# Cross-attention on one core: where the row-maximum steps stand in the score phase

## What is computed

```
qn = layernorm(x);  q = qn @ Wq / 8;  k, v = split(media @ Wkv)      # 16 heads of 64
sim  = where(mask, q @ k.T, lowest)                                   # 256 x 1601 for each head
attn = softmax(sim);  x = x + tanh(gate) * (attn @ v) @ Wo
x = x + tanh(ff_gate) * gelu(layernorm(x) @ W1) @ W2
# second layer: softmax attention over the raw media, a sigmoid gate, an RMS norm
```

## Time and profile before

| | |
|---|---|
| median of 3 runs | 872.42 us (lowest 872.27, highest 2096.33) |
| span of the profiled execution | 870.5 us; the time around it is not listed apart |
| TensorE matmul busy | 833.8 us, 96% |
| TensorE weight load busy | 699.4 us, 80% |
| VectorE busy | 587.1 us, 67% |
| ScalarE busy | 464.3 us, 53% |
| GpSimd busy | 401.1 us, 46% |
| all row-maximum reductions (L901) | 256, 245.4 us |

### The profile page before, as it was taken

How to read it: one execution, slowest core, us unless ns; L and a number is a source line. 1 busy time by engine, 2 the same in 40 slices (tenths; PEclk the granted TensorE clock), 3 DMA queues, 4 the chain that set the end, 5 groups by cost and what they waited for, 6 DMA issues and landing times.

```text
span 870.5 us, 18230 instructions
## 1 busy us (share of the span) xinstructions
PE 833.8 (96%) x7777; PEld 699.4 (80%) x7777; DVE 587.1 (67%) x968; ACT 464.3 (53%) x727; POOL 401.1 (46%) x189
## 2 busy tenths in 40 slices
PE   4999999999999999999999999999999999998986
PEld 3788878888888788888888888888888778887775
DVE  6856788867567888675677886756788622126375
ACT  4755655657356566573566665735555441126352
POOL 2445565655625656556256565562566650000002
PEclk9999999999999999999999999999999999999999
DMA  9000001000000010000000000000000700000201
GB/s 285 23 1 2 2 2 39 2 2 2 2 1 2 4 37 1 2 2 2 2 1 2 2 1 2 2 2 2 1 2 4 214 1 1 1 1 1 76 1 48
DMA packets 20559, 16.80 MB, mean 19 GB/s; under 512 B 1008, under 2 KB 19456, under 8 KB 20480
## 3 DMA queue, kind: packets, MB, share of 16 engines
q1 hardware_dynamic: 20192, 15.38, 6.0%
q10 hardware_dynamic: 288, 0.27, 0.1%
HBM read 14.59 MB, written 1.05 MB: 18 GB/s over the span
## 4 chain that ended last, share of the span: by engine, by line
PE 78%; DVE 12%; ACT 5%; POOL 2%; issue 1%; DMA 1%; ACTq 0%; POOLq 0%; DVEq 0%
PE psum L1284 21%; PE psum L1298 17%; PE psum L345 13%; PE psum L1253 6%; PE psum L1209 4%; PE psum L1313 3%; PE psum L1060 3%; PE psum L1074 3%; PE psum L1148 2%; DVE mx L901 2%; DVE k_lo L890 2%; DVE ot L931 1%; PE psum L1304 1%; ACT k_hi L608 1%; POOL acc L450 1%
## 5 line engine op out<-in xcount | busy, mean ns | idle before, releaser
L450 POOL TENSOR_TENSOR acc<-acc,ring 128x1024 f32<-128x1024 f32 x128 | 306.7, 2396 | 18.7 <-POOL acc L445 0.5
L901 DVE TENSOR_REDUCE mx<-psum 128x2 f32<-128x800 f32 (+2 forms) x256 | 245.4, 989 | 86.6 <-PE psum L1253 74.7
L631 ACT ACTIVATE ring<-psum 128x1024 f32<-128x1024 f32 x192 | 197.0, 1027 | 64.5 <-PE psum L1284 58.0
L445 POOL TENSOR_TENSOR acc<-ring 128x1024 f32<-128x1024 f32 x32 | 76.9, 2404 | 274.4 <-ACT ring L631 274.4
L1298 PE MATMUL psum<-ring,v 128*64 128x256 f32 (+1 forms) x1664 | 186.7, 381 | 1.7
L1298 PEld LDWEIGHTS psum<-ring,v 128*64 128x64 f32 (+1 forms) x1664 | 116.6, 137 | 61.1 <-DVE k_lo L890 3.9
L1284 PE MATMUL psum<-nm,maskrow 64*128 64x256 f32 (+1 forms) x832 | 123.9, 294 | 0.6 <-ACT ring L631 0.6
L1284 PE MATMUL psum<-q_lo,k_hi 64*128 64x256 f32 (+1 forms) x832 | 116.9, 278 | 0.0
L1284 PE MATMUL psum<-q_hi,k_hi 64*128 64x256 f32 (+1 forms) x832 | 116.8, 277 | 0.0
L1284 PE MATMUL psum<-q_hi,k_lo 64*128 64x256 f32 (+1 forms) x832 | 116.5, 277 | 0.0
L623 ACT COPY od<-psum 128x512 f32<-128x512 f32 x32 | 18.8, 588 | 167.8 <-PE psum L1304 167.8
(11 more groups left out here) (150 smaller groups left out, 1351.4 us busy)
## 6 DMA issues: line engine op xcount, KB each, us to landing
nat<-in_ctx_dram SPq DMA_DIRECT2D x7, 768.0 KB
w<-in_L_xattn_W_dram SPq DMA_DIRECT2D x2, 1024.0 KB, 8.7
wo<-in_L_xattn_Wo_dram SPq DMA_DIRECT2D x1, 1024.0 KB, 9.7
out_dram<-t_res SPq DMA_DIRECT2D x8, 128.0 KB, 1.7
mask<-in_mask_BxS_bk_dram SPq DMA_DIRECT2D x4, 200.1 KB, 7.1
nat<-in_ctx_dram SPq DMA_DIRECT2D x2, 384.0 KB, 7.3
ring<-in_L_xattn_Wkv_dram SPq DMA_DIRECT2D x2, 384.0 KB, 6.2
wq<-in_L_xattn_Wq_dram SPq DMA_DIRECT2D x1, 768.0 KB, 6.7
```

Of the source, the lines that this page charges most:

```text
L445: nc.gpsimd.tensor_tensor(acc[:, :, :, :], ring[:, 0, :, :, :], ring[:, 1, :, :, :], ALU.add)\
L450: nc.gpsimd.tensor_tensor(acc[:, :, :, :], acc[:, :, :, :], ring[:, g, :, :, :], ALU.add)\
L631: nc.scalar.activation(ring[:, g, :, :, :], score_set[m % 2].rearrange("p (h i q) -> p h i q", h=2, i=2), ACT.Exp).then_inc(S["p_ready"], 1)
L901: nc.vector.tensor_reduce(mx[:, t, :, c], pair[:, :, 0:min(c1, KEYS) - c0], axis=AX.X, op=ALU.max).then_inc(S["m_max"], 1)
```

## The change

Only the order of the score phase. Before: M0, S0, M1, M2, S1, M3, S2, M4, S3, M5, S4, M6, S5, M7, S6. After: M0, S0, M1, S1, M2, S2, M3, S3, M4, S4, M5, S5, M6, S6, M7.

```diff
 def row_phase(j):
-    out = [("M", j + 1, 0), ("S", j, 0), ("M", j + 1, 1)]
-    for g in range(1, KEY_GROUPS):
-        out += [("M", j + 1, g + 1), ("S", j, g)]
-    return out
+    out = []
+    for g in range(KEY_GROUPS):
+        out += [("M", j + 1, g), ("S", j, g)]
+    return out + [("M", j + 1, SCORE_STEPS - 1)]
```

## The result

The changed kernel takes 893.80 us (median; 892.99 to 894.67) against 872.46 for the one before: a ratio of 1.0244, 95% interval 1.0232 to 1.0257. That is 21.3 us slower, where +7.5 was forecast and 888 was the upper end. The span is 892.9 us, against 870.5. One execution of the kernel before took 2096.33 us, for a reason that nothing here shows; without it that kernel's median is 872.42.

A forecast was written before the change was run, and what follows sets the result against it. TensorE, busy 96% of the span, was taken as the bound, with 16.2 us of waits as the ceiling of any gain. Terms 3.5 + 4.6 + 0.4 − 0.1 − 0.4 − 0.5 = +7.5 gave 879.9 us, range 873 to 888.

The forecast's parts named there:

- costed at nothing: N ends 0.46 us later, K 0.29; 0.28 of cover, 0.17 used, at most +2 us if the cover is gone.
- The sum of the waits for banks: Over the 31 score phases, gains at the start and later bank releases at the end together give +7.5 us.
- (a) to (f): The 31 score phases sorted by which bank wait ends them; in order +3.5, +4.6, +0.4, −0.1, −0.4, −0.5 us.
- The head's wait: At M2, TensorE's wait for its bank goes: 0.26 us usually, 0.4 to 0.6 in late phases, 0.9 in one.
- The alternation of the exponentials: Within the score phase, exponentials hold S2 and S4 instead of S3 and S5; such groups take 1.05 us.
- Term (f): The phase at 679.71, entered with VectorE late: an estimate of −0.5 us, with ends of −1.1 and 0.
- The clock: TensorE's clock stays at 1.00 through the new waits of 0.5 to 1.3 us, so no cost.
- A: The gain at the phase start stays and items behind the phase do not wait: −8.5, 864 us; chance 0.06.
- C: M6 comes at 6.87 because the exponential does not hold S2 and S4: +2, 874.5 us; chance 0.15.
- B: VectorE's lateness reaches TensorE everywhere; full phases follow N, every phase pays 0.46 us: +13.4, 886 us; chance 0.17.
- The sign that the prediction named for B: The full phases between R and N grow as well; no size given for the sign itself.
- The rule on rotating PSUM banks: Skill advice to overlap evacuation with the next matmuls; taken alone, a gain of 0.26 us or more per phase.

The follow-up runs named there:

- the profile with the reduction: The changed order with N's negation (L910) written as a tensor_reduce over an axis of length one instead of a tensor_scalar: 879.82 us, ratio 1.0086 to before.
- the end alone and the tensor_scalar: The kernel before with only the last two steps reordered (S6 then M7), N's negation left as it was: 905.23 us, ratio 1.0376.
- the head alone: The kernel before with only the phase start reordered (M0 S0 M1 S1 M2 S2 M3), N's negation as a reduction: 867.30 us, ratio 0.9940.
- the end alone: The kernel before with only the last two steps reordered (S6 then M7), N's negation as a reduction: 881.09 us, ratio 1.0097.

## Why the prediction was wrong

**The step that failed** is the one on N under "costed at nothing". It gave N 0.28 us of cover and used 0.17 of it, taking N's own length as fixed. Measured, the length of its second instruction depends on GpSimd: 0.23 us in the gap between two additions, up to the rest of a 2.4 us addition outside it. The same paragraph said that GpSimd's chain ends earlier and took that for harmless. It is half of the cause: N moved 0.45 later (9.17 to 9.62, medians) and the chain 0.45 earlier in the phase (4.14 to 3.69), together 0.9 us, and the gap that N had been hitting is 0.14 us wide. Neither shift was mis-sized. The paragraph asked of each engine's queue whether it was late, not what else two engines share. That N had been hitting the gap at all was luck of the old order. Price: 14.0 us, from the two forms of one instruction in the same order (893.80 and 879.82).

**The sum of the waits for banks was right.** Forecast +7.5 us, measured +7.4 with N's wait away. Phase by phase, in the profile with the reduction, its terms (a) to (f) are 3.1, 4.7, 0.2, −0.1, −0.4 and −0.4, in sum 7.1, where 3.5, 4.6, 0.4, −0.1, −0.4 and −0.5 were forecast; that the total agrees to 0.1 is partly luck. M6 was put at 7.10 and M7 at 7.83, the next item at 8.56 and M7's pair free at 9.46; the profile has 7.07 to 7.10, 7.78 to 7.79, 8.52 to 8.56 and 9.43 to 9.44. One figure of the prediction does not fit its own places: the period of two groups is 2.37 by them (M4 at 4.73, M6 at 7.10), and 2.35 to 2.37 in the profile, not 2.24; the sum does not use it. The head's wait is gone: the 12.5 + 3.7 us of the earlier trace rows are 1.1 + 0.6, all of it in the first list, and in their place stand waits of 25.9 us in 37 cases behind the phases, on the weight-load side (15 to 25 were forecast, in 22 or more; 3.8 in 7 cases stood there before); the two largest rows:

```profile
PEld psum L345 <- DVE mx L901: 8.4, 11, 1.6
PEld psum L1209 <- DVE mx L901: 8.4, 11, 1.6
```

The alternation of the exponentials came too, S2 and S4 long at 0.92 to 0.94 and S3 at 0.84 to 0.86 from first to last matmul. Term (f), −0.5, was right without N's wait (−0.4: 8.47 + 6.26 in place of 9.57 + 5.52). In the changed kernel it turned into +2.6, which the forecast's bound of 0 had excluded.

**The clock** was costed at nothing. That held for the waits that were forecast, and not for one place that was not. In the last batch's sixth full phase R, not K, waits for N. One microsecond windows of the changed kernel:

```profile
709.00:710.00 1.00, 0.02 (x1) 0.00 (x0) 0.97 (x2) 1.00 (x4) 1.00 (x1) 1.00 0.65 158
710.00:711.00 1.00, 0.19 (x1) 0.22 (x2) 1.00 (x2) 0.55 (x2) 0.86 (x2) 0.91 0.09 23
711.00:712.00 1.00, 1.00 (x6) 1.00 (x7) 1.00 (x4) 0.37 (x1) 1.00 (x1) 0.50 0.05 11
...
713.00:714.00 1.00, 1.00 (x4) 0.82 (x4) 0.36 (x1) 0.77 (x1) 0.86 (x2) 0.50 0.07 16
714.00:715.00 1.00, 1.00 (x6) 0.84 (x5) 0.00 (x0) 0.24 (x1) 1.00 (x1) 0.88 0.00 0
```

TensorE does nothing for 1.80 us (709.01 to 710.81), and then runs at 0.50 of its clock (1.2 instead of 2.4 GHz) until after 714. That full phase takes 9.20 us against 6.26 with the reduction, 2.9 more, about twice what N's 1.3 us alone would make, so some 1.6 of the 14.6 us by which the full phases of the two profiles differ are the clock's (an estimate). The waits of 0.5 to 1.3 us, which were the ones forecast, left the clock at 1.00 in this kernel. Other runs show that the length of one wait does not decide it: with the end alone and the tensor_scalar, the clock fell during TensorE waits of 1.14, 1.46, 1.57 and 1.80 us or up to 0.9 us behind them, and not at two other waits of 1.57.

**The rivals.** A (the spacing is all, 864) is out: phases end at 8.5, not at 8.1. C (no net effect) is out: M6 came at 7.1. B (VectorE's lateness reaches TensorE) named the right place, the instructions behind N, but a price of 0.46 in every phase. Against the same order with the reduction it was 1.3 in five of the six third and fourth phases of the body and 1.7 in one, 0.7 in the three eighth phases, 0.3 to 0.4 in four fifth ones, 2.9 in one, and nothing in the other 17. The sign that the prediction named for B, full phases that grow, came true, by another mechanism than B's. The range ended at 888, and 0.05 was left for times above 890, because no case in it let an instruction of VectorE grow. The prediction also called 2% about what a measurement can tell; the 95% interval of the ratio is 0.25% wide.

**The rule on rotating PSUM banks** was weighed rightly: alternation did end the wait at the head, and the last evacuation cost more than that gave. What the order itself is worth without N's wait is seen in the four orders with the reduction: 867.3 with the head alone, 872.5 with none, 879.8 with head and end, and 881.1 with the end alone. The two parts do not add up: −5.2 and +8.6 would be +3.4, and the whole is +7.4.

## What to carry to other kernels

When a change shifts one engine's work against another's, look not only for queues and waits but for an instruction whose duration depends on what runs beside it. The minimum, median and maximum of each short instruction show it before anything is changed: L931 had 424, 948 and 2478 ns. Here a 0.23 us instruction sat in a 0.14 us gap between 2.4 us additions of the other engine, pair after pair, and moving it by 0.9 us cost 14 us. In these profiles such a wait has no row of its own in the list of waits; it stands in the length of the instruction. A short instruction in front of TensorE's work should not be of the kind that waits for the other engine; a reduction over an axis of length one did the same job here without waiting. And an alternation of producer and consumer must be judged at its last step too, where the evacuation has nothing behind it.

## What the runs showed of the hardware

A VectorE tensor_scalar from SBUF to SBUF (128 x 128, one input) that starts inside a GpSimd tensor_tensor (128 x 1024, 2.4 us) ends 0.08 to 0.09 us behind it (31 of 32 in the changed kernel, 1.47 to 1.96 us long; 0.23 us outside an addition). A VectorE tensor_reduce of the same size from the same tensor takes 0.29 us beside the same addition, in the 31 pairs that have one, against 0.23 for the tensor_scalar when it is free. A VectorE tensor_tensor with two inputs in SBUF (128 x 256, 0.42 us) that starts inside such an addition ends 0.28 to 0.29 us behind it (25 of 27 in the kernel before). A later start of GpSimd made this kernel faster (893.8 to 880.1).
